# A radix threshold search on one Trainium2 core: counts and group matrix as rounded operands, and the reached candidate taken by a maximum

## The reference

```python
probs = softmax(xf @ Wr)                       # 4096 tokens, 8 experts
topk_probs, topk_experts = top_k(probs, 2)
cap = ceil(4096 * 2 * 1.25 / 8)                # 1280 slots for each expert
for e in range(8):
    mask = topk_experts == e
    gate = sum(where(mask, topk_probs, 0.0), axis=-1)
    g_masked = where(any(mask, axis=-1), gate, -inf)
    vals, idx = top_k(g_masked, cap)           # the cap largest gates of this expert
    g = where(isfinite(vals), vals, 0.0)
    h = relu(xf[idx] @ W1[e]) @ W2[e]
    y = y.at[idx].add(g[:, None] * h)
```

## Time and profile before

| | |
|---|---|
| median of 3 executions | 1224.91 us (1223.55 to 1226.75) |
| the profiled execution, its own time | 1222.99 us |
| its span, first to last instruction | 1221.2 us |
| mean granted TensorE clock | 0.938 of 2.4 GHz |
| TensorE busy | 1123.6 us (92%) |
| VectorE busy | 820.2 us (67%) |
| ScalarE busy | 420.5 us (34%) |
| GpSimd busy | 546.0 us (45%) |

### The profile page before, as it was taken

How to read it: one execution, slowest core, us unless ns; L and a number is a source line. 1 busy time by engine, 2 the same in 40 slices (tenths; PEclk the granted TensorE clock), 3 DMA queues, 4 the chain that set the end, 5 groups by cost and what they waited for, 6 DMA issues and landing times.

```text
span 1221.2 us, 16986 instructions
## 1 busy us (share of the span) xinstructions
PE 1123.6 (92%) x5754; PEld 974.4 (80%) x5754; DVE 820.2 (67%) x1549; ACT 420.5 (34%) x762; POOL 546.0 (45%) x403
## 2 busy tenths in 40 slices
PE   7999999499999999999985548999999999999996
PEld 5878888388888888887775447889898989899996
DVE  5576999579999999999576785454444444444442
ACT  5321222223333333331562212343443534344432
POOL 3130000177777777774000022566565656565723
PEclk8999999799999999999985557999999999999998
DMA  7100022343111011002440212754544443534322
GB/s 263 35 35 1 1 52 50 104 142 102 32 32 32 32 32 32 32 21 69 139 144 7 100 56 68 192 146 68 134 91 117 83 121 79 132 73 78 60 42 27
DMA packets 69633, 93.35 MB, mean 76 GB/s; under 512 B 5668, under 2 KB 57636, under 8 KB 69592
## 3 DMA queue, kind: packets, MB, share of 16 engines
q1 hardware_dynamic: 51576, 60.96, 15.9%
q0 software_dynamic: 18016, 31.86, 13.6%
HBM read 65.29 MB, written 23.31 MB: 73 GB/s over the span
## 4 chain that ended last, share of the span: by engine, by line
PE 83%; DVE 7%; issue 2%; ACT 2%; DMA 2%; POOL 2%; SPq 0%; DVEq 0%; POOLq 0%; ACTq 0%
PE ps L1436 27%; PE ps L1575 18%; PE ps L1591 12%; PE ps L1592 6%; PE ps L1386 5%; PE ps L1375 4%; PE ps L1356 4%; PE ps L1464 2%; DVE arena L1141 1%; PE ps L1557 1%; PE ps L1485 1%; DVE qkv L819 1%; DMA qkv<-in_w 1%; PE ps L1537 1%; DVE arena_rounded L819 1%
## 5 line engine op out<-in xcount | busy, mean ns | idle before, releaser
L1575 PE MATMUL ps<-arena_rounded,w_high 128*128 128x384 f32 (+1 forms) x768 | 211.4, 356 | 2.1 <-DVE arena_rounded L819 2.1
L578 POOL TENSOR_TENSOR kv_low<-arena,kv_high 128x512 fp32r<-128x512 f32 x128 | 187.1, 1491 | 38.7 <-ACT kv_high L630 38.7
L1436 PE MATMUL ps<-kv_high,toep_high 128*128 128x512 f32 (+1 forms) x512 | 193.9, 379 | 11.1 <-POOL kv_low L578 11.1
L1436 PE MATMUL ps<-kv_low,toep_high 128*128 128x512 f32 (+1 forms) x512 | 193.9, 379 | 0.0
L1436 PE MATMUL ps<-kv_high,toep_low 128*128 128x512 f32 (+1 forms) x512 | 193.0, 377 | 0.0
L1258 DVE SCALAR_TENSOR_TENSOR hidden_low<-ps,hidden_high 128x384 fp32r<-128x384 f32 (+1 forms) x192 | 115.6, 602 | 100.1 <-ACT hidden_high L788 99.7
L602 POOL DMA_INDIRECT out<-arena x80 | 126.2, 1578 | 105.1 <-DVE arena L819 97.4
L591 POOL DMA_INDIRECT qkv<-row_scratch,arena x80 | 82.6, 1033 | 185.3 <-DVE arena L1212 159.2
L1575 PEld LDWEIGHTS ps<-arena_rounded,w_high 128*128 128x128 f32 x768 | 140.4, 190 | 13.4 <-issue 2.5
L819 DVE TENSOR_TENSOR arena<-qkv 128x512 f32 (+1 forms) x128 | 136.8, 1127 | 12.5 <-SPq L339 12.5
L788 ACT ACTIVATE hidden_high<-ps 128x384 fp32r<-128x384 f32 (+1 forms) x192 | 101.3, 528 | 126.7 <-PE ps L1575 126.7
(11 more groups left out here) (194 smaller groups left out, 1954.2 us busy)
## 6 DMA issues: line engine op xcount, KB each, us to landing
arena<-ssm_scratch SPq DMA_DIRECT2D x32, 320.0 KB, 3.2
qkv<-in_w SPq DMA_DIRECT2D x16, 512.0 KB, 5.1
qkv<-in_w SPq DMA_DIRECT2D x8, 1024.0 KB, 8.8
arena<-in_u SPq DMA_DIRECT2D x7, 1024.0 KB, 6.2
row_scratch<-qkv SPq DMA_DIRECT2D x4, 1056.0 KB, 4.6
qkv<-arena SPq DMA_DIRECT2D x16, 256.0 KB, 3.4
row_scratch<-arena SPq DMA_DIRECT2D x4, 1024.0 KB, 6.4
out<-qkv SPq DMA_DIRECT2D x4, 1024.0 KB, 9.3
```

The costliest lines, as they stand in the source:

```text
L578: nc.gpsimd.tensor_tensor(kv_parts[s][1][:, quarter], kv_flat[s][:, quarter], kv_parts[s][0][:, quarter].bitcast(F32), ALU.subtract).then_ ...
L1436: last = mm(ps[:, 4 * s + g, (lo - 2 * g) * B * 64:BANK], toep_parts[s][a][:, o * P:(o + 1) * P], kv_parts[s][x][:, src], start=n == 0 and ...
L1575: last = mm(ps[:, f % 4, 0:width], w1_parts[q][a][:, dc * F + f * P:dc * F + (f + 1) * P], xeT_parts[x][dc][:, 0:width], start=dc == 0 and ...
```

## The change

Four edits belong together:

- `count` becomes a 128 x 4 tile of type float32r (the rounded fp32 operand of TensorE); its fourth column is set once from `eps`. ScalarE makes a float32r copy of `group_ones`, `group_ones_r`, ahead of `y_turned(0)`. The products of lines 1520 and 1523 use these two, with four columns.
- `reached` becomes (sums >= 1280) * `cand`, three values, one scalar_tensor_tensor that reads PSUM and `cand`, without a sum.
- `accepted` becomes the maximum of the three, a tensor_reduce. It holds a whole candidate and not a digit only; as `cand` contains `theta`, the later ORs give the same bits.
- The constant `digit_unit` and its load go; the waits on `consts_in` count seven loads.

```diff
-        "digit_unit": np.tile((4.0 ** np.arange(BITS // 2 - 1, -1, -1)).astype(np.float32), (P, 1)),
+        group_ones_r = arena_r[:, KK0 + 3968:KK0 + 3968 + P]
-        digit_unit = sb("digit_unit_sb", [P, BITS // 2])
-        digit = sb("digit", [P, 1])
-        count = sb("count", [P, 3])
+        count = sb("count", [P, 4], F32R)
+        ones_ready = sem("ones_ready")
...
-                              (digit_unit, "digit_unit"), (expert_id, "expert_id"),
+                              (expert_id, "expert_id"),
...
+            act.wait_ge(consts_in, 16 * 7)
+            copy(group_ones_r, group_ones[:]).then_inc(ones_ready, 1)
             y_turned(0)
...
+            nc.vector.tensor_copy(count[:, 3:4], eps[:])
             nc.vector.memset(theta[:], 0)
...
-                    link(nc.vector.tensor_scalar(reached[:], ps[:, 1, 0:3], float(CAP), None, ALU.is_ge, ALU.add, accum_out=digit[:]))
-                    link(nc.vector.tensor_scalar(accepted[:], digit[:], digit_unit[:, bass.ds(n, 1)], None, ALU.mult))
+                    link(nc.vector.scalar_tensor_tensor(reached[:], ps[:, 1, 0:3], float(CAP), cand[:].bitcast(F32),
+                                                        ALU.is_ge, ALU.mult))
+                    link(nc.vector.tensor_reduce(accepted[:].bitcast(F32), reached[:], AX.X, ALU.max))
...
+            pe.wait_ge(ones_ready, 1)
             for i in range(BITS // 2):
                 pe.wait_ge(count_ready, i + 1)
-                mm(ps[:, 1, 0:3], group_ones[:], count[:], start=True, stop=True).then_inc(count_psum, 1)
+                mm(ps[:, 1, 0:4], group_ones_r, count[:], start=True, stop=True).then_inc(count_psum, 1)
                 rows_back(i + 1)
             pe.wait_ge(count_ready, BITS // 2 + 1)
-            mm(ps[:, 1, 0:1], group_ones[:], count[:, 0:1], start=True, stop=True).then_inc(count_psum, 1)
+            mm(ps[:, 1, 0:4], group_ones_r, count[:], start=True, stop=True).then_inc(count_psum, 1)
```

More of the change, by code:

```diff
@@ L481, in _ @@
             sp.wait_ge(mod_out, 16)
-            sp.wait_ge(consts_in, 16 * 8)
+            sp.wait_ge(consts_in, 16 * 7)
             sp.wait_ge(fold_ready[1], UNITS)
@@ L964, in _ @@
             dve.sem_inc(mod_ready, 1)
-            dve.wait_ge(consts_in, 16 * 8)
+            dve.wait_ge(consts_in, 16 * 7)
             qkv_rows(B - 1, 0)
```

## The result

The changed kernel takes 1220.4 us (median of 9 executions, 1217.71 to 1221.17) against 1226.25 us of the kernel before, measured beside it. The ratio is 0.9953, 95% interval 0.9945 to 0.9962: faster by 0.47%, which is 5.8 us. The kernel before, in one of its 9 executions there, took 1316.28 us; the ratio leaves that one out. A second timing of the same changed kernel (e5) gave 0.9956 (0.9943 to 0.9969).

A forecast was written before the change was run, and what follows sets the result against it. TensorE made up 83% of the chain, but the search was taken as bound by a VectorE-TensorE ring of 2.72 us a round. Savings of 5.55 + 0.22 = 5.8 us gave 1219.1 us, range 1216.3 to 1222.8.

The forecast's parts named there:

- The product, 0.22 us a round: Search's count product, 15 times: one rounded matmul replaces a pair, ending 0.22 us earlier; bounds nothing and 0.24 us.
- VectorE in time: In a search round, `base` ends 0.07 us before `reached` could start, so the shortened product stays the later.
- `reached` and `accepted`, 0.10 + 0.05: Search round on VectorE: `reached` without a sum saves 0.10 us, `accepted` by a maximum 0.05 us, 15 times each.
- The search as a whole: All 15 search rounds: product, `reached` and `accepted` together save 0.37 us a round, 5.55 us.
- The product behind the search: Line 1523, after the search: the product ends 0.22 us earlier, and idle time before `need` covers the whole gain.
- What is added: Ahead of the search: the copy into the fourth column and ScalarE's rounding fall into idle time; uncovered, the copy costs 0.16 us.
- It reaches the end: From the search to the kernel's end: a microsecond saved in the search was expected to reach the end.
- The clock: Start of the expert products: the clock's rise may shift, 3.1 us won or lost; about 1 us in a median.
- closed ring: Search round: VectorE and TensorE wait on each other in turn, six links adding to 2.72 us, expected to become 2.35.

The follow-up runs named there:

- e5: The changed kernel as it is, timed a second time beside e6 and e7 on the same chip; 1220.23 us, ratio 0.9956 to the kernel before.
- e1: Changed kernel with the old `reached`, `accepted` and `digit_unit` put back, so only the count product is changed; ratio 0.997 to the kernel before.
- e2: Kernel before with only the new `reached` and `accepted` instructions, its count product left plain fp32; ratio 0.9973 to the kernel before.
- e3: Changed kernel with the maximum taken three times in each round, each linked, same result; ratio 1.0006 to the kernel before.
- e4: Changed kernel with 16 unread TensorE products, 12 before the second one-hot product and 4 after the first row transposes; 1217.21 us, ratio 0.9934.
- e6: e4 with a third burst of 7 unread products before the first row transposes and 5, not 4, in the last; 1216.92 us, ratio 0.9934.
- e7: e6 plus unread plain fp32 products around the router's last batch, 5 before its transposes and 2 before its products; 1220.17 us, ratio 0.9958.

## Why the prediction came out right

The forecast was 1219.1 us, 5.8 us below the median known then (0.47%); measured are 0.9953 and 1220.4 us, where the kernel before has 1226.25. The difference is right to 0.1 us, closer than it can be measured (the interval leaves 4.7 to 6.7 us): the parts below add to 6.3 us in the traces, not 5.8, so this closeness is partly luck. The absolute time is 1.3 us off, because the kernel before came out 1.3 us above the 1224.91 from which I worked.

- *The product, 0.22 us a round.* Right: 0.22 in e1 and in the changed kernel. Both readings behind it were good: the first matmul of the pair as a stand-in for a lone one, and the spacing of 32.
- *VectorE in time.* Right, and as narrow as worked out: from the end of `base` to `reached` it is 0.08 us (forecast 0.07), and 0.04 us of it lie before the product's end.
- *`reached` and `accepted`, 0.10 + 0.05.* 0.11 + 0.06 measured, as the spacing of small linked instructions is 0.19 and not 0.20 us. In 15 rounds that makes 2.56 us for 2.25. By the Trainium skill, "VectorE: DVE Perf Modes", section "Rules for kernel authors", the reduce was a risk; for three elements it took 0.16 us, as much as any other small instruction here.
- *The search as a whole.* 5.55 us forecast, 5.79 measured.
- *The product behind the search.* 0.22 us forecast and seen (from it to the next product 1.42 us, was 1.64). Another 0.23 us came unforeseen between the two products of line 1526, now 3.32 us apart (was 3.55): the idle 0.26 us before the VectorE instruction of line 1162 is gone. It belongs to the two new VectorE instructions and not to the product: the same spacing is 3.32 us in e2 and 3.70 in e1 (702.81 to 706.51 us).
- *What is added.* The copy into `count` takes 0.15 us and VectorE still idles 0.37 us behind it; the rounding takes ScalarE 0.29 us, and it still idles 14.30 us behind it. Both cost nothing, as said.
- *It reaches the end.* Shown by e3, 6.5 us (about 5 to 8) for 6.60, and by the medians of the change itself, 5.8 us.
- *The clock.* The warning was needed for reading the traces, not the times: one trace against one trace gives 2.0 us, the medians 5.8. That the low level lies over the start of the experts and costs about 3 us was worked out from the earlier trace rows as an uncertainty; e4 and e6 show that it can be won, e7 that it need not be. I had not thought of it as an offer.

The milestones: the first gather was expected near 718.5 and starts at 719.82, the first expert product near 734.6 and starts at 735.87. Both are late by 1.3 us: the search starts 1.81 us late, and 0.5 us more than forecast were saved since.

What stays open: by what the new VectorE instructions remove the idle 0.26 us before line 1162, which lies behind them, and why a turn of the loop costs about 0.35 us in the kernel before, the changed kernel, e1 and e2 alike, and 0.90 and 0.61 in e3. No run shows the mechanism of either.

## What to carry to other kernels

A closed ring between two engines is priced link by link, from start to start in one turn's timeline; the sum times the number of turns gave 5.55 of 5.79 us here, from a stretch that is 3% of the span. Rounded operands save a weight load and a matmul even where the moving side has four columns; the values here are small whole numbers (counts up to 256 and ones), and no run tries others. When TensorE must wait ahead of dense work, products nobody reads can be put into the wait to have the clock up in time, which gave 3.3 us in e6. They need to fit into the gap at the low level, and what waits behind them counts: those ahead of the transposes in e7 held up ScalarE by 2.7 us. Two single traces should not be subtracted from each other, but compared stretch by stretch.

## What the hardware showed that I had not expected

- The granted clock differs between executions of the same instructions. Between 650 and 652 us it was 1.00 in one trace of the changed kernel and 0.50 in the other (e5), and the first count product starts at 664.23 and at 666.34 us.
- The last 32 router matmuls of 8 columns, issued back to back, ran at 1.2 GHz from end to end in e5 (7.00 us). In e6, whose instructions are the same up to there, they took 4.45 us: the clock had risen just before them (0.63 from 648 to 650 us, 1.00 from 650 to 652) and fell again before they ended. In e4 it rose at the end of 12 products of 512 columns, and it fell again during 32 matmuls of 70 columns.
- Behind `reached`, `accepted` and `cand` of the changed kernel the linked next instruction starts 0.19 to 0.20 us later, whether the first compares and multiplies, reduces or ORs; with a sum written out it was 0.30, with a per-partition operand 0.25. `base`, whose operand is picked by the round's number, starts 0.31 us behind `theta`.
- The turn of the hardware loop on VectorE costs 0.37 and 0.35 us in the kernel before, and 0.90 and 0.61 us in e3, which has only two more instructions in each round.
